# Order of weight loads, rank counts and GpSimd fetches in the expert stage of an attention and mixture-of-experts kernel

## The reference

```python
xn = xf / rms * norm_weight
probs = softmax(xn @ router_weight.T + router_bias)
_, idx = top_k(logits.T, 512)                     # 512 tokens for each of 16 experts
xe = xn[idx]
h = gelu(einsum('ecd,efd->ecf', xe, fc1_weight) + fc1_bias[:, None, :])     # 256 -> 1024
y = einsum('ecf,edf->ecd', h, fc2_weight) + fc2_bias[:, None, :]            # 1024 -> 256
contrib = y * gates[:, :, None]
output = zeros.at[flat_idx].add(contrib)          # then divided by the sum of a token's gates
x = x + output
```

## Time and profile before

| | |
|---|---|
| median of 3 runs | 1071.66 us (1070.63 to 1072.16) |
| profiled execution | 1070.8 us, its span 1069.1 us |
| TensorE busy, share of the span | 83% |
| VectorE, ScalarE, GpSimd busy | 73%, 47%, 56% |
| mean granted TensorE clock | 0.919 of full speed |
| data moved | 159.94 MB, 150 GB/s in the mean |

### The profile page before, as it was taken

How to read it: one execution, slowest core, us unless ns; L and a number is a source line. 1 busy time by engine, 2 the same in 40 slices (tenths; PEclk the granted TensorE clock), 3 DMA queues, 4 the chain that set the end, 5 groups by cost and what they waited for, 6 DMA issues and landing times. The chain is left out here.

```text
span 1069.1 us, 20303 instructions
## 1 busy us (share of the span) xinstructions
PE 888.5 (83%) x6023; PEld 702.0 (66%) x6023; DVE 781.3 (73%) x1688; ACT 500.6 (47%) x887; POOL 599.8 (56%) x565
## 2 busy tenths in 40 slices
PE   3888999999999999998720017889998999999996
PEld 3656766667666766676410015778988888889985
DVE  4667878887888888887379975676777777777653
ACT  1444556555655566555230002544555555655532
POOL 3246556655565656565661045376766666776535
PEclk9889999999999999999655558989999999999998
DMA  4334555565556555564250015155555455555633
GB/s 155 133 140 170 207 193 189 197 213 185 201 184 224 184 205 187 207 212 158 83 172 8 0 36 149 55 158 153 146 152 142 143 147 147 160 167 155 159 68 40
DMA packets 110061, 159.94 MB, mean 150 GB/s; under 512 B 19380, under 2 KB 76980, under 8 KB 109896
## 3 DMA queue, kind: packets, MB, share of 16 engines
q1 hardware_dynamic: 94408, 133.78, 36.1%
q0 software_dynamic: 15616, 25.70, 10.8%
HBM read 66.55 MB, written 26.28 MB: 87 GB/s over the span
## 5 line engine op out<-in xcount | busy, mean ns | idle before, releaser
L527 DVE TENSOR_REDUCE NM<-bank 128x4 f32<-128x480 f32 x256 | 159.6, 655 | 58.2 <-PE bank L637 58.0
L370 ACT ACTIVATE PT<-bank 120x512 f32<-120x512 f32 x256 | 139.0, 595 | 69.8 <-PE bank L662 69.0
L311 POOL TENSOR_SCALAR XN<-X,mv,rstd 128x256 f32<-128x256 f32 x128 | 155.3, 1221 | 6.9 <-POOL rstd L306 6.1
L1488 PE MATMUL bank<-W2H,HH 128*128 128x256 f32 x512 | 145.9, 285 | 3.6 <-issue 3.5
L1490 PE MATMUL bank<-W2H,HL 128*128 128x256 f32 x512 | 144.5, 282 | 1.3 <-issue 1.3
L1489 PE MATMUL bank<-W2L,HH 128*128 128x256 f32 x512 | 144.4, 282 | 1.1 <-issue 1.0
L978 POOL DMA_INDIRECT out_dram<-C,IO x60 | 111.2, 1854 | 52.3 <-issue 29.2
L637 PEld LDWEIGHTS bank<-KX,QX 128*128 128x128 f32 x512 | 73.5, 197 | 63.9 <-issue 31.4
L1244 DVE TENSOR_TENSOR HL<-hf,HH 128x512 fp32r<-128x512 f32 x128 | 86.2, 691 | 40.0 <-ACT HH L1399 27.8
L637 PE MATMUL bank<-KX,QX 128*128 128x240 f32 x512 | 104.8, 319 | 11.5 <-issue 6.3
L1394 ACT ACTIVATE hf<-bank,B 128x512 f32<-128x512 f32 x128 | 87.9, 689 | 55.4 <-PE bank L1490 45.8
(11 more groups left out here) (176 smaller groups left out, 1779.4 us busy)
## 6 DMA issues: line engine op xcount, KB each, us to landing
QX<-QH SPq DMA_DIRECT2D x64, 256.0 KB
W<-w1T_dram SPq DMA_DIRECT2D x16, 1024.0 KB
W<-w2T_dram SPq DMA_DIRECT2D x16, 1024.0 KB
KX<-KH SPq DMA_DIRECT2D x64, 240.0 KB, 2.3
X<-x_dram SPq DMA_DIRECT2D x32, 256.0 KB, 2.8
QX<-QL SPq DMA_DIRECT2D x32, 256.0 KB
RC<-PVS SPq DMA_DIRECT2D x32, 256.0 KB, 2.4
OC<-PVS SPq DMA_DIRECT2D x32, 256.0 KB, 2.6
```

What stands on the lines that cost most here:

```text
L311: ins = pool.tensor_scalar(dst[:, t, :], src[:, t, :], mv[:, t, 0:1], rstd[:, t:t + 1], ALU.subtract, ALU.mult)
L370: act.activation(PT[u][0:M, HE * k:HE * (k + 1), :], score_bank[k % 2][0:M, :], ACT.Exp, scale=SCALE) \
L527: dve.tensor_reduce(NM[u][:, t, :].rearrange("p (f n e) -> p n e f", n=HN, e=HE)[:, n, :, :], smax_bank[q % 2][:, 0:4 * M].rearrange("p (e ...
L1488: pe.matmul(o, wh, xh, start=first, stop=False)
```

## The change

There are three edits. SyncE's loads are in another order: expert 2's W1 also waits until expert 1's gather has landed (`gathered[1]`), and from there on the W1 of expert e + 1 is loaded ahead of the W2 of expert e, instead of behind W2 and the bias of e. VectorE counts the ranks of expert 1 (`find_first(1)`) ahead of the columns of expert 0. GpSimd, in the part of its stream ahead of its loop, waits at ten places until an earlier fetch or add has landed (`landed`).

```diff
--- before.py
+++ after.py
@@ -936,17 +936,18 @@
                 .then_inc(slot_stored, 16)
         sp.wait_ge(early_stored, 64)
         sp.wait_ge(slot_stored, 16 * NC)
+        sp.wait_ge(gathered[1], 16 * GT)
         load_1(2)
-        load_2(2)
-        load_b(2, 0)
-        load_1(3)
-        load_2(3)
-        load_b(3, 1)
-        with sp.Fori(2, E // 2) as i:
+        with sp.Fori(1, E // 2 - 1) as i:
             for u in range(2):
-                load_1(2 * i + u)
+                load_1(2 * i + (u + 1))
                 load_2(2 * i + u)
                 load_b(2 * i + u, u)
+        load_1(E - 1)
+        load_2(E - 2)
+        load_b(E - 2, 0)
+        load_2(E - 1)
+        load_b(E - 1, 1)
 
     @block.gpsimd
     def _(pool):
@@ -1004,6 +1005,10 @@
 
         pool.wait_ge(first_stored, 16 * FE)
         pool.wait_ge(row_ready, 1)
+
+        def landed(done, count):
+            pool.wait_ge(done, 16 * GT * count)
+
         lookup(FR[0], first_ranks, row_of[:, 0, :], first_ranked[0])
         lookup(FR[1], first_ranks, row_of[:, 1, :], first_ranked[1], range(GT // 2))
         pool.wait_ge(idx_ready, 1)
@@ -1013,19 +1018,29 @@
         lookup(XG[1], xn_table, II[1], gathered[1])
         pool.wait_ge(early_stored, 64)
         pool.wait_ge(probs_ready, 1)
+        landed(gathered[1], 1)
         ranks(1, 0)
-        for u in range(2):
-            lookup(first_rows[u], slot_table, row_of[:, u, :], first_gated[u])
+        landed(ranked[0], 1)
+        lookup(first_rows[0], slot_table, row_of[:, 0, :], first_gated[0])
+        landed(first_gated[0], 1)
+        lookup(first_rows[1], slot_table, row_of[:, 1, :], first_gated[1])
         gather(1, 0)
+        landed(gathered[0], 2)
         ranks(1, 1)
+        landed(ranked[1], 1)
         pool.wait_ge(slot_stored, 16 * NC)
         ranks(2, 0)
+        landed(ranked[0], 2)
         gather(1, 1)
+        landed(gathered[1], 2)
         ranks(2, 1)
         add_up(0, 0, True)
+        landed(added, 1)
         gather(2, 0)
+        landed(gathered[0], 3)
         ranks(3, 0)
         add_up(0, 1, False)
+        landed(added, 2)
         gather(2, 1)
         with pool.Fori(2, E // 2 - 2) as i:
             ranks(i + 1, 1)
@@ -1305,8 +1320,8 @@
         next_rows(0, 0)
         next_rows(1, 1)
         dve.wait_ge(c_loaded, 32)
+        find_first(1)
         columns(0, 0)
-        find_first(1)
         dve.wait_ge(table_ready, 1)
         dve.sem_inc(y0_ready, 1)
         for f in range(KF):
```

## The result

| | before | changed |
|---|---|---|
| median of the runs, us | 1071.14 (4 runs, 1065.09 to 1072.16) | 1054.74 (4 runs, 1049.05 to 1055.39) |
| profiled execution, us | 1070.8 | 1055.39 |
| its span, us | 1069.1 | 1053.7 |

The ratio is 0.9856, with a 95% interval from 0.9816 to 0.9896. The change makes the kernel faster by 15 to 16 us (11 to 20 by the interval). The prediction was 1050.7 us with a range of 1045.5 to 1060: the direction and the range hold, and the time is 4 us longer than forecast, for a reason that is worth following.

What follows compares the result with a forecast made beforehand. TensorE was busy 888.5 of 1069.1 us, so a change is worth what it takes from the gaps in its stream. 4 + 6 + 2 + 9 = 21 us off the median 1071.66 gave 1050.7 us, range 1045.5 to 1060.

Steps and rivals of the forecast that it cites:

- W1 a turn ahead, steady part: Eleven steady turns: ScalarE no longer waits for W1 nor TensorE for XTL; 9 us gained, bounds 6 and 10.
- W1 was not what held the steady turns: Rival, steady turns: something else sets XTL, so the 9 us stay and the time is 1059.7 us; 10%.
- W1 a turn ahead, start of the loop: Turn to expert 3: its W1 issued near 682.5, one 1 MB transfer left beside the gather; 6 us, bounds 0 and 7.
- The trickle stays: Rival, loop start: "issue" gaps and late "done" belong to the code's first pass; 6 and 2 fall away, 1058.7 us; 14%.
- Expert 1's ranks first: Stage entry: expert 1's gather moves up 3.9 us, ahead of W1, and expert 1 starts earlier; 4 us, bounds 1 and 5.
- SyncE's wait for the gather: Stage entry: expert 2's W1 load moves from 652.90 to about 655, its split comes 28 us later; nothing.
- GpSimd's waits: Ahead of the loop: ten added waits cost 0 if a fetch lands in about 2 us, with 3 to 4 us slack.
- the rival of 6%: GpSimd's waits cost 4.4 us each, TensorE waits 11 us once, the loop behind gains the rest back; 1061.7 us; 6%.
- The next turn: Turn from 726.59 to 753.64, 27.05 us long, 3.5 above 23.51: 2 us gained, bounds 0 and 3.5.

Runs made afterwards that it cites:

- e10: The changed kernel without the two waits on adds, with the old order of loads and no wait of SyncE; 1055.17 us, ratio 0.9982.
- e3: The kernel before with only the count of expert 1's ranks ahead of expert 0's columns; 1070.16 us, ratio 1.0022.
- e4: The kernel before with only GpSimd's ten waits, old loads and old order of columns and ranks; 1069.70 us, ratio 1.0023.
- e2: The kernel before with only the new order of the weight loads, without the wait for expert 1's gather; 1054.73 us, ratio 0.9883.
- e1: The changed kernel without all ten of GpSimd's waits; 1057.88 us, ratio 0.9901.
- e7: The changed kernel with only the first three of GpSimd's ten waits, the other seven gone; 1050.32 us, ratio 0.9890.
- e11: The changed kernel without the two waits on adds, W1 of expert 3 still behind expert 2's W2, early W1 from expert 4; 1044.54 us, ratio 0.9887.
- e12: The changed kernel without the two waits on adds, with expert 0's columns ahead of expert 1's ranks as before; 1044.71 us, ratio 0.9871.
- e6: The changed kernel without SyncE's wait for expert 1's gather; 1051.16 us, ratio 0.9885.
- e8: The changed kernel run once more, unchanged, in a later group; 1050.77 us, ratio 0.9863.
- e5: The changed kernel without GpSimd's two waits for adds to land; 1042.58 us, ratio 0.9803.
- e9: The changed kernel without the two waits on adds, expert 2's gather issued first and W1 of expert 3 behind it; 1042.49 us, ratio 0.9860.

## Why the prediction was right, and where it was not

**W1 a turn ahead, steady part: right.** Forecast 9 us, bounds 6 and 10. ScalarE's wait for W1 and TensorE's for XTL are gone in every kernel with the new loads and there in e10, which puts it down to the load order. Eleven turns take 257.6 to 260.1 us in eight of the ten traces with the new loads, 268.6 before and 268.5 in e3, 266.7 and 267.0 in e4 and e10, so 6.5 to 11. The changed kernel's own two traces (262.7, 262.8) gain only 5.9, for a reason that has nothing to do with W1: two of the eleven turns are long in each, 26.1 and 25.1 us in the first, 25.5 and 26.5 in the second, against 23.4 otherwise, and in each of the four VectorE or ScalarE got TensorE's signal 2 to 5 us late. The prediction put the release of W2's buffer a good 15 us behind that of W1's; in its own trace it is 10 us (the remainder of W1 ends at 800.5, W2 is issued at 810.39) and in the changed kernel 11. The size of the step does not hang on it.

The turn of 26.1 us, on VectorE's timeline of the changed kernel:

```profile
765.62 1.41 DVE L1248 TENSOR_SCALAR XTH<-bank,NW 128x512 fp32r<-128x512 f32 x2 [5.94 <-remote]
```

The eight transposes that it waited for had ended at 761.0. The split of the columns starts 4.6 us after them, without a releaser inside the core.

**The rival "W1 was not what held the steady turns" falls.**

**W1 a turn ahead, start of the loop: right in size, wrong in its reason.** Forecast 6, measured 6.8 (31.4 to 24.6), in the place that was named: W1 issued at 680.27 (forecast 682.5), transposes at 706.22 (707.6), no gaps with "issue". But the step said that the trickle would go because one 1 MB transfer instead of two would lie there. e2, which has the loads alone, keeps it at a DMA share of 0.46; e1 and e7 keep it too. It is absent in all nine traces that have GpSimd's middle waits (in e4 and e10 even with the old loads). Of the five kernels without them, four have it; e3 is the exception. So the trickle goes with how many of GpSimd's fetches are queued at once; e3, with just as many, has only two gaps of 0.91 and 0.49 us, so they are not the whole cause. The term thus hung as much on the step that I priced at nothing, and neither edit has it alone: in this turn the waits without the new loads gain 1.7 and 2.8 us (e4, e10), the loads without the middle waits at most 1.4 (31.0, 32.2 and 30.0 in e1, e2 and e7). The loads are needed, by e4, e10 and e11, above all for a reason that the step did not name for this turn: W2 and W1 issued together delay expert 3's gather, for which TensorE then waits 2.88 to 3.45 us and loses its clock. Had the change come without the waits, the forecast would have been 6 us too good here. "The trickle stays" was ruled out by the result, with an argument that did not carry: that it was not the code's first pass was right (every kernel here runs that code for the first time there), that it was the transfers was not. The Trainium skill's page "Runtime: NRT & Kernel Launch", section "Instruction fetch mechanics", which the prediction named beside this rival, is not decided by these runs: the queue of fetches and the trickle change together, and no trace shows what TensorE's sequencer waited for.

**Expert 1's ranks first: about right in sum, but not alone.** Forecast 4 (the working gave 4.6), measured 4.9 to the start of expert 1 (19.2 us after expert 0's first product before, 14.3 now) and 6.0 to that of expert 2. The gap of 2.0 us ahead of expert 1 that the step foretold is there, 1.99 us, and so is the half clock behind it. The reason holds too, the gather no longer lies beside W1; but e12 shows that SyncE's wait alone does nearly that, so the 4.9 us can't be booked to the ranks alone. What the step did not see is that the early gather also sets GpSimd free to pile up fetches. Without its waits (e1, e3) expert 2 starts 5 us later than in the kernel before. I had looked for what an early transfer collides with, and priced the wait, but not what the missing wait lets loose.

**SyncE's wait for the gather: right, nothing, but only beside early ranks** (e6 against e8). With late ranks it is worth most of the entry: expert 1 starts 15.4 us after expert 0 in e12 and 21.5 in e4.

**GpSimd's waits: this step failed.** It said 0, on the ground that four adds take four times 1.85 us and their pauses, and land in 1.9 us like a lookup. Both figures were too small for these four. The fourth takes 4.93 us to issue, and lands only 4.6 us after that, so that the next fetch starts 9.5 us after its start (in e8 the issue takes 2.35 and the landing 6.4, which makes 8.7); the gather for expert 4 was thus only issued from 727.65 on, instead of landing near 729.5. The trace of the kernel before could have warned: its adds have a mean of 1.85 us, but one takes 4.63 (at 979.96). And the fourth add of expert 0 takes 2.35 to 4.98 us in the nine traces with GpSimd's middle waits and 1.56 to 2.01 in the five without, so the waits may themselves have made it longer. The slack of 3 to 4 us was used up, and the turn that should have gained 2 us lost 2.6. e5, without the two waits, has that turn at 23.7: the waits cost 6 us in the turn, and 8.2 us in the median beside e8 (by the traces 2.7 lie in the steady part, where e8 has late signals, for which the waits need not be the reason). The 6 us alone are more than the 4 by which the forecast was too good. The chain "TensorE waits once, the loop behind gains the rest back" is the rival of 6%, nearly as it was written (11 us at 4.4 us each), but it came at one wait and not evenly at six.

**The next turn: forecast 2, lost.** Where the adds don't stand in the way, it takes 23.4 to 24.1 us (e1, e5, e7, e9 to e12) against 27.0: 3 to 3.5 were there to be had, my upper bound. e10 is among them with the old loads, and e1 and e7 with the trickle, so it was neither the crowded transfers nor the trickle. The kernel before, e2 and e3 have no waits on adds either, and take 27.0, 26.1 and 25.3 us; there ScalarE and VectorE got TensorE's signal 3.7, 5.4 and 1.8 us late at its head.

**Behind expert 15, a cost that nobody named: 1.5 us.** Near the end TensorE is idle for 1.99 us in every trace that I compared, and in seven of the fourteen (before, e1, e2, e3, e5, e7, e9) it goes on at full clock. In the changed kernel the granted clock falls behind that gap (0.60 in the window at 1010, against 1.00 in e2's) and the tail is 48.4 us long instead of 46.9. It did so in seven of the nine traces with GpSimd's middle waits (all but e5 and e9) and in none of the five without them, so it may belong to the change; why a wait 300 us earlier should matter there, the runs don't tell.

**The sum.** Forecast 4 + 6 + 2 + 9 = 21; measured 6.0 + 6.8 - 2.6 + 5.9 - 1.5 = 14.6, and 0.8 from ahead of the stage. That the sum came out within 4 us is in part luck. Two errors of the same source partly cancelled: without GpSimd's middle waits most of the 6 us at the start of the loop would not have come, and its waits on adds took 6 to 8; I had priced both at nothing. The range was also set a little wide below: the terms' own upper bounds, 5 + 7 + 3.5 + 10, reach down to 1046.2 and not to 1045.5.

**A better version came out of it.** e5, the change without the two waits on adds, has a ratio of 0.9803 against 0.9863 for the change beside it: 8.2 us less by the medians. e9 reaches the same median, 1042.5, on another chip, and its stage is 1.1 us shorter; the two were not run beside each other, so which is better is open. No kernel yet has the short entry of e9 (37.7), the short turn to expert 3 of e8 (23.6) and the steady 257.6 together.

## What to carry to other kernels

When a step becomes early, ask what used to hold back the engine behind it: here GpSimd's wait for row numbers had, unnoticed, kept its fetches from piling up. A wait is then priced in both directions, what it delays and what it keeps from being queued, and it is put where the next thing needed soon is a fetch, not behind an add whose landing nothing needs before the next adds, a turn later. For one wait take the duration of that instruction in that place: the mean over sixty of its kind hid ones of 4.6 us before the change and 4.9 after it, and an add's landing is not a lookup's. And a load whose buffer comes free early should not stand in its queue behind one whose buffer comes free late.

## What the runs showed of the hardware that I had not expected

- **TensorE's results reach the other engines late at times.** An engine stands idle with its input finished, 1 to 5 us and longer, with no releaser inside the core. In the changed kernel TensorE's last matmul of a product ended at 713.02 and ScalarE began at 715.82. ScalarE's idle time of this kind at the entry is 7.28 us in e3, 5.91 in e1 and 5.15 in e2, which have no waits of GpSimd there; none of the ten traces with the entry waits has one of that length there. Later in the stage it comes with and without waits, and it costs the turn between nothing and 3 us (2.7 us late in e5, and the turn takes 23.7; 4.6 us late in the changed kernel, and the turn takes 26.1, against 23.4). e9 to e12 have none at all, and they ran on the chip on which the kernel before was faster too (1056.88); e4, on another, has none either. Whether this is what makes chips differ is open.
- **A trickle of TensorE that is no wait for data.** One matmul in 0.5 to 1 us for some 6 us (11 in 6 us in e2), at a DMA share of 0.46, in four of five kernels without GpSimd's middle waits and, at that place, in none of nine with them. It follows the queue of indirect fetches rather than the large transfers, but not strictly: e4, with all waits, has a short one in a later turn (gaps of 0.70, 1.04 and 0.33 us at 764 to 766). The records of the instruction queue's own fetches show none longer than 2.11 us near it (at 706.29, before; 0.92 to 1.23 in e1, e2 and e7) and none at all in e4 between 744 and 776. Why TensorE's sequencer should feel GpSimd's queue is open: no run changed that queue alone by degrees.
- **The landing of a gather depends on when it meets a 1 MB load.** From the end of the last issue of expert 2's gather to the transposes that wait for it are 4.8 us in e8, 5.0 in e6 and 3.8 in e12, where W1 was issued at most 1.1 us from that last issue, and 1.9 to 2.0 in the other traces in which TensorE stood waiting a microsecond or more for it.
- **The fourth indirect add of a group** took 4.93 us to issue in the changed kernel, 4.91 in e5 and 2.35 in e8, its three predecessors about 1.6 each. Over the fourteen traces it is 1.56 to 4.98 us. Its landing took another 4.6 us in the changed kernel and 6.4 in e8, where a lookup with nothing beside it lands in 1.9.
- **The same gap drops the clock or doesn't.** After the 1.99 us of idle near the end the granted clock of the next 3 us was 0.60 in the changed kernel and 1.00 in e2, and the tail 1.5 us longer or not. The same gap thus cost its 2 us in seven traces and 1.5 us more in the other seven.
